# More row tiles of attention weights made ahead, a join taken five groups later, and a gradient product split around the last scan of a graph network

## What is computed

```python
def get_H(xx):
    z = xx @ W_fc.T
    e = jax.nn.sigmoid(jnp.concatenate([z[src], z[dst]], axis=-1) @ W_attn.T)
    emax = jax.ops.segment_max(e, dst, num_segments=n)
    w = jnp.exp(e - emax[dst])
    denom = jax.ops.segment_sum(w, dst, num_segments=n)
    h = jax.ops.segment_sum(w / denom[dst] * z[src], dst, num_segments=n)
    h1 = jax.ops.segment_sum((h @ W_encK.T + b_encK)[src], dst, num_segments=n)
    K = _mlp3(h1, K_w0, K_b0, K_w1, K_b1, K_w2, K_b2)
    ue = (h @ W_p1.T + b_p1)[src] + (h @ W_p2.T + b_p2)[dst]
    U = _mlp3(ue, U_w0, U_b0, U_w1, U_b1, U_w2, U_b2)
    return jnp.sum(jax.ops.segment_sum(K[src] * U, dst, num_segments=n))
dHdx = jax.grad(get_H)(x)
return dHdx @ J.T - dHdx @ D.T
```

## Time and profile before

| | |
|---|---|
| median of three runs | 9449.99 us (9428.79 to 9453.63) |
| profiled execution, time | 9455.71 us |
| its span | 9453.9 us |
| mean granted TensorE clock | 0.689 of full speed |
| PE busy | 4884.9 us (52%) |
| DVE busy | 4608.6 us (49%) |
| ACT busy | 2818.8 us (30%) |
| POOL busy | 5441.5 us (58%) |
| DRAM read and written | 1606.44 MB and 711.62 MB |

### The profile page before, as it was taken

The page is one execution under the profiler, slowest core; times in us unless marked ns, Lnnn a source line. Parts: engine busy times, 40 slices in busy tenths (PEclk is TensorE's granted clock), DMA queues, the critical chain, the costliest instruction groups (busy, mean ns, idle before and its releaser), DMA issues.

```text
span 9453.9 us, 77287 instructions
## 1 busy us (share of the span) xinstructions
PE 4884.9 (52%) x27914; PEld 2630.0 (28%) x27914; DVE 4608.6 (49%) x6100; ACT 2818.8 (30%) x2192; POOL 5441.5 (58%) x5420
## 2 busy tenths in 40 slices
PE   1000007999457777775577756344430035038976
PEld 0000006888113233231222222244430023032333
DVE  5789746777000000000398950488875410428870
ACT  0111110000000000000298940366657500429850
POOL 4777777777777777777610027688877777320000
PEclk6555555555578988987798975667665568559986
DMA  8887216444598989999799999455559848538767
GB/s 188 307 299 236 53 52 138 148 148 153 207 414 358 414 361 377 399 362 415 267 285 268 283 219 365 139 201 203 201 212 373 308 151 340 183 84 285 262 223 291
DMA packets 1203136, 2404.24 MB, mean 254 GB/s; under 512 B 566439, under 2 KB 818794, under 8 KB 1171354
## 3 DMA queue, kind: packets, MB, share of 16 engines
q1 hardware_dynamic: 996986, 2076.35, 61.8%
q0 software_dynamic: 187136, 170.29, 6.9%
q10 hardware_dynamic: 18720, 153.79, 4.2%
HBM read 1606.44 MB, written 711.62 MB: 245 GB/s over the span
## 4 chain that ended last, share of the span: by engine, by line
POOL 37%; DMA 26%; issue 12%; PE 11%; ACT 7%; ACTq 4%; DVE 2%; SPq 1%; DVEq 1%; POOLq 0%
POOL arena L486 18%; DMA arena<-cells_w 14%; POOL xd L489 9%; POOL cells_w L489 9%; DMA arena<-cells_c 8%; PE ps L699 5%; ACT arena L1031 3%; ACTq L1030 3%; ACT arena L1029 2%; PE ps L788 2%; DMA arena<-hot 1%; PE ps L880 1%; ACTq L2271 1%; PE ps L1162 1%; PE ps L1054 1%
## 5 line engine op out<-in xcount | busy, mean ns | idle before, releaser
L699 PE MATMUL ps<-arena 128*64 128x458 f32 (+2 forms) x7252 | 1345.0, 653 | 663.1 <-DMA arena<-cells_w 661.6
L486 POOL DMA_INDIRECT arena<-t_a,arena x832 | 947.9, 1139 | 1090.8 <-DMA t_a<-arena 837.7
L1054 PE MATMUL ps<-arena 128*33 128x400 f32 x6336 | 1173.1, 525 | 297.7 <-DVE arena L1049 289.8
L489 POOL DMA_INDIRECT sorted<-arena x832 | 843.8, 1014 | 289.9 <-issue 289.9
L489 POOL DMA_INDIRECT xd<-arena x832 | 832.0, 1000 | 260.9 <-issue 253.2
L717 DVE COPY carry<-ps 64x128 f32<-64x128 f32 (+1 forms) x5 | 1.5, 296 | 2006.1 <-PE ps L699 2006.1
L489 POOL DMA_INDIRECT cells_c<-arena x832 | 810.4, 974 | 293.5 <-issue 293.5
L486 POOL DMA_INDIRECT arena<-t_kv,idx x832 | 826.3, 993 | 258.7 <-issue 252.9
L489 POOL DMA_INDIRECT cells_w<-arena x832 | 813.7, 978 | 276.6 <-issue 276.6
L699 PEld LDWEIGHTS ps<-arena 128*64 128x64 f32 (+1 forms) x7252 | 425.5, 147 | 1579.0 <-issue 813.2
L1054 PEld LDWEIGHTS ps<-arena 128*33 128x33 f32 x6336 | 368.3, 115 | 1100.3 <-issue 662.9
(11 more groups left out here) (536 smaller groups left out, 9104.9 us busy)
## 6 DMA issues: line engine op xcount, KB each, us to landing
arena<-cells_w SPq DMA_DIRECT2D x245, 3200.0 KB
arena<-cells_c SPq DMA_DIRECT2D x294, 800.0 KB, 6.2
arena<-cells_turned SPq DMA_DIRECT2D x200, 800.0 KB, 8.2
cells_w<-arena SPq DMA_DIRECT2D x49, 3200.0 KB, 22.2
weighed_cells<-arena SPq DMA_DIRECT2D x68, 1600.0 KB, 14.2
arena<-weighed_cells SPq DMA_DIRECT2D x68, 1600.0 KB, 7.2
cells_c<-arena SPq DMA_DIRECT2D x50, 1600.0 KB, 5.8
cells_turned<-arena SPq DMA_DIRECT2D x100, 800.0 KB, 5.4
```

The lines of the kernel that those rows point to most:

```text
L486: return pool.indirect_dma_start(dst, None, table, bass.IndirectOffsetOnAxis(ap=index, axis=0))
L489: return pool.indirect_dma_start(table, bass.IndirectOffsetOnAxis(ap=index, axis=0), source, None)
L699: mm = pe.matmul(bank[base + k][g * f:(g + 1) * f, 0:m], rows_of, tile[:, g * width + at:g * width + at + m], start=first, stop=last, skip ...
L1054: last = pe.matmul(bank[4 * h + c][64 * kind:64 * kind + 33, 0:400], own[:, t, :], moving[:, 400 * c:400 * c + 400], start=t == 0, stop=do ...
```

## The change

Three tables or constants and two pieces of code change. `BEFORE` becomes 23 tiles spread over the 50 (0, 3, 5, 7, 9, 11, 14 and so on to 48). The join moves from group 29 to 34 of the puts and the fetch of `gk` from 37 to 42. ACT makes the tanh of the next piece between the exponential and the square of the present one. The gradient product is split: `DFM1` and `SUMS3` are multiplied right after the quarters, ahead of the join of the last scan, into four banks of PSUM that the scan's masks don't use; the product with `DFM2` is added after the scan.

```diff
-        BEFORE = range(0, NT, 3)
+        BEFORE = [t for t in range(NT) if t * 23 % NT < 23]
...
-        ALIAS_AT, XK_AT, GK_AT, HD_AT = 768, 15, 37, 29
+        ALIAS_AT, XK_AT, GK_AT, HD_AT = 768, 15, 42, 34
...
+        def gradient_pe(pe, source, weight, first):
+
+            if not first:
+                pe.wait_ge(S["fm_taken"], STEP["dhf"])
+            for t in range(NT):
+                to = bank[4 + t // 16][:, t % 16 * 32:t % 16 * 32 + 32]
+                g, at = t // (NT // 2), t % (NT // 2) * P
+                a = slice(64 * g, 64 * g + 64)
+                if t == NT // 2:
+                    last.then_inc(S["group_done"], 1)
+                    groups_done[0] += 1
+                    pe.wait_ge(S["group_done"], groups_done[0])
+                last = pe.matmul(to, source[a, at:at + P], weight[a, :], start=first and t % 16 == 0, stop=not first,
+                                 skip_group_check=True)
+                if first:
+                    last = pe.matmul(to, SUMS3[0:96, t * P:t * P + P], fold[32][0:96, 0:32], start=False, stop=False,
+                                     skip_group_check=True)
+                elif t % 16 == 15 or t == NT - 1:
+                    last.then_inc(S["fm_made"], 1)
...
+            tanh_act(0)
+            for i in range(len(todo)):
                 act.drain()
                 act.wait_ge(S["weighed"], base + max(0, 2 * i - 1))
-                act.activation(AHEAD_EXP, tanh, ACT.Exp, scale=0.5, bias=half[:]).then_inc(S["weights_made"], 1)
+                act.activation(AHEAD_EXP, AHEAD_TANH[i % 2], ACT.Exp, scale=0.5, bias=half[:]).then_inc(S["weights_made"], 1)
+                if i + 1 < len(todo):
+                    tanh_act(i + 1)
                 act.wait_ge(S["weighed"], base + 2 * i)
-                act.activation(AHEAD_SQUARE, tanh, ACT.Square).then_inc(S["weights_made"], 1)
+                act.activation(AHEAD_SQUARE, AHEAD_TANH[i % 2], ACT.Square).then_inc(S["weights_made"], 1)
...
-            for made, t, got in node_banks("dhf", 32, bank):
+            for made, t, got in node_banks("dhf", 32, bank[4:8]):
...
             quarters_pe(pe)
+            await_made(pe, "dh_made")
+            gradient_pe(pe, DFM1, WD1, True)
             ends_pe(pe, "dsum", OD, 64, bank[3])
             await_made(pe, "dd_made")
             to_features_pe(pe, "DD", nodes(DD, 64), 4)
-            await_made(pe, "dh_made")
-            to_nodes_pe(pe, "dhf", DFM1, 64, 32, lambda c: WD1[64 * c:64 * c + 64, :], bank,
-                        more=((DFM2, 64, lambda c: WD2[64 * c:64 * c + 64, :]), (SUMS3, 96, lambda c: fold[32][0:96, 0:32])))
+            gradient_pe(pe, DFM2, WD2, False)
```

More of the change, by code:

```diff
@@ L1094, in ahead_act, with tanh_act @@
             base = 4 * NS
-            for i, j, phase, t, h in ahead():
+            todo = list(ahead())
+            def tanh_act(i):
+                _, j, phase, t, h = todo[i]
                 if j % len(BEFORE) == 0 and h == 0:
                     act.wait_ge(S[f"other{phase}"], 16 * 2)
-                tanh = AHEAD_TANH[i % 2]
-                act.activation(tanh, piece_of(AHEAD_OTHER[phase], h), ACT.Tanh, bias=a_dst[:, t:t + 1])
+                act.activation(AHEAD_TANH[i % 2], piece_of(AHEAD_OTHER[phase], h), ACT.Tanh, bias=a_dst[:, t:t + 1])
+            tanh_act(0)
+            for i in range(len(todo)):
                 act.drain()
                 act.wait_ge(S["weighed"], base + max(0, 2 * i - 1))
-                act.activation(AHEAD_EXP, tanh, ACT.Exp, scale=0.5, bias=half[:]).then_inc(S["weights_made"], 1)
+                act.activation(AHEAD_EXP, AHEAD_TANH[i % 2], ACT.Exp, scale=0.5, bias=half[:]).then_inc(S["weights_made"], 1)
+                if i + 1 < len(todo):
+                    tanh_act(i + 1)
                 act.wait_ge(S["weighed"], base + 2 * i)
-                act.activation(AHEAD_SQUARE, tanh, ACT.Square).then_inc(S["weights_made"], 1)
+                act.activation(AHEAD_SQUARE, AHEAD_TANH[i % 2], ACT.Square).then_inc(S["weights_made"], 1)
         def ahead_dve(dve):
```

## The result

| | before | changed |
|---|---|---|
| median of the runs | 9444.13 us (4 runs, 9428.79 to 9453.63) | 9369.1 us (4 runs, 9359.15 to 9382.79) |
| ratio, 95% interval | | 0.9921 [0.9907, 0.9934] |
| profiled execution, span | 9455.71, 9453.9 us | 9359.15, 9357.3 us |
| mean granted TensorE clock | 0.689 | 0.692 |

A forecast was written before the change was run, and what follows sets the result against it. POOL's puts bound the time to 8142 us, then a serial scan, join and gradient product, then ACT in the back stage. Gains of 54.7 and 22, together 76.7 us, off the median 9449.99 gave 9373 us, range 9350 to 9424.

The forecast's parts named there:

- The gradient product: Between last scan and back stage: two of three products move ahead of the scan, 54.7 us less (50 to 55).
- The weights ahead: Stage making weights early: 24 more pieces at DMA's pace, 6.20 us each, ending about 7654; ACT's new order worth nothing.
- The join: Join among POOL's puts: five groups later, 7604.4 to 7709.3; DVE has 55 us left, less the last write; cost nothing.
- The cost of nothing for the last put: End of POOL's puts: same transfers in another order, so the last put still lands at 8142.78.
- The quarters: Before the last scan: preparation ends at 8137.4 against the last put at 8142.78, slack shrinking from 110 to 5.3 us.
- The bound upwards of 20 us: Most that late quarters were allowed to cost at the scan's start; the cost itself was taken as 0.
- The back stage: Two phases after the gradient product: PE leads at 5.44 us a tile; 10 and 12 less, together 22, at most 26.
- The rival of a limit at 349: Back stage gains nothing because DMA scaled to share 1 allows only 349 GB/s; time 9395 us, chance 0.16.
- Late quarters: Before the last scan: quarters overrun their 5.3 us slack; at 25 us delay the scan loses 20; 9393 us, chance 0.12.
- The slower case: Back stage held by DMA at 284 GB/s: 9509 us; slower than before if below 311 GB/s; chance 0.04.
- the change might not do what it says: Moved gradient products would run only after the scan, gaining nothing there; 9428 us with the back stage's gain, chance 0.03.
- the two middle cases: No gain in the back stage (0.16) and late quarters (0.12): 9393 to 9395 us, both together 9415.

## Why the prediction was right

**The gradient product: -54.7 forecast, -56.5 measured in the trace.** The row taken for the remaining product, `GK` with 21.80 us, was 2 us too dear: it took 19.74. The clock tells why. `GK` had run at 0.50 from end to end. Here the granted clock was 1.00 from 8398 to 8400, 0.99 from 8400 to 8402 and 0.50 from 8402 on, so the 0.83 in the window above is a mean of the two levels, 2.4 and 1.2 GHz. It fell though PE was busy without a break from 8400 to 8404, and stayed down while PE was busy for 5.94 of the 6 us from 8404. The first 50 matmuls took 8.83 us and the other 50 took 10.88. PE had been idle for 70.10 us ahead of the turn; the upper level came during the turn and was lost 2.3 us into the product. The prediction's "all through this product" is not exact for the same reason: the product before stood at 1.00 from 8414 to 8416 and at 0.50 only from 8418. By the rule of the Trainium skill that was weighed there (TensorE: Matmul & The Clock Gate, "What's actually happening") a busy array has 2.4 GHz, and the product would have taken an estimated 10.9 us; the trace speaks against it here as it did before.

**The weights ahead: 6.20 us a piece forecast, 6.23 measured;** ACT's order at nothing, and nothing it was, by the run with the old order.

**The join: "slack 55 less the last write".** DVE was idle 41.36 us before it, and POOL's loss in it was 3.2 us, as costed. The difference from 55 is not the write. DVE's pieces ended at 7652.7, as forecast (7654), but the join came some 15 us before 7709, because the puts began 18.4 us earlier. With the join back at 29 the loss is 70.7, which is the price that the move avoids. Two readings of POOL's stream were wrong without touching the sum: 750 of the 832 puts lie between 7082 and 8142 (they began at 6955.24), and from the first to the last put there are 885 indirect transfers, before and now, not 982. The cost of nothing for the last put was short by 1.8 us, the longer landing.

**The quarters: 5.3 us of slack forecast, 9.2 measured.** The positions have to be corrected for the puts, which began 18.4 us earlier in this execution: the end of the preparation, forecast at 8137.4, becomes 8119.0, and it was 8117.88; the last put, 8142.78 before, becomes 8124.4, and it had landed at 8127.06. So 1.1 us of the larger slack is the quarters' and 2.7 the last put's. The bound upwards of 20 us was not needed, and the run with two more groups shows that it was the right thing to bound: past the slack the scan starts as much later as the quarters end later.

**The back stage: -22 forecast, -22.0 measured, and part of that agreement is luck.** The prediction took four of the 100 pieces as done at 8543.04. It was five: the records before it are 32, 32 and 16, and a piece has 16. So 95 pieces were left, 258.4 us of PE's time and not 261.1, and its own rule with 2 us of waits gives 12.9 less, not 10. From the same piece on, phase 0 now runs from 8471.09 to 8731.46, 260.4 against 273.3: 12.9 less. (From its second tile, 8458.06, it is 273.4 against 286.7 from 8529.65: 13.3 less.) Phase 1 went from 285.8 to 277.0, 8.7 less, 12 forecast: "with 2 us of waits" was too hopeful there, where 5 are left. PE waits for DVE and DVE for counts. With the pieces counted right the sum of the two phases would have been 25; the miscount of 3 us one way and the waits of 3 us the other cancel in the 22. Waits from 8471 to 8725 us:

```profile
DVE arena L1063 <- DMA arena<-cells_turned: 51.5, 18, 4.9
...
PE ps L1074 <- DVE arena L1069: 6.2, 5, 2.1
```

That PE would lead with 5.44 us a tile was right (two pieces of 2.70 where nothing makes it wait), and that the reads "just fit" as well: share 0.99 to 1.01 at 350 to 358 GB/s. The rival of a limit at 349 fell. Its ground was that the rate ends at a share of 1 and grows in line with it; the share went to 1.05, and with 27 tiles the same reads reached 382. The 358 GB/s of the Trainium skill (DMA: Bandwidth & Descriptors, "Where 436 GB/s comes from"), with its estimate of 272 us a phase, could not be told from PE's own 272 at 23 tiles. At 27 tiles the windows of 374 to 382 GB/s are above it, and the measurement decides.

**The other rivals.** Late quarters (slack used up) appear at place 36 and not at 34. The slower case needed less than 311 GB/s; the stage moved 350 to 358. That the change might not do what it says is excluded by PE's rows at 8117.50 and 8172.59.

The chances do not quite add up: the forecast and the two middle cases are 0.88 by themselves, and they were given as 0.87 with a part of the rest.

What the sum left out is the 15.7 us at the start. The changed kernel's profiled execution, which shows them, is 10 us under its own median. Of the signs named ahead, "the scan's first load still within a few us of 8143" missed by 16 for this reason. That forecast and median agree to 4 us is finer than these runs can tell, as they spread over 24. Why the puts begin earlier in one execution than in another was not looked into.

## What to carry to other kernels

Cost an edit between fixed points of the trace (here from the turn to the first matmul, and from there to the second turn), not by where things stand on the clock: positions moved by 18 us between executions of the same code, while of those stretches the first agreed to 0.1 us between kernels with the same product, and the second to 5 us. Work that is moved ahead of a stage must be paid for on every queue that it passes: without the five groups by which the join was moved, POOL would have stood for 70 us behind DVE. And when work is made ahead and read back, stop where the engine that then leads has no waits left: here 20 of 50 tiles did for PE what 23 did, with fewer reads.

## What the runs showed of the hardware that was not expected

- TensorE's granted clock fell from 0.99 (8400 to 8402 us) to 0.50 (8402 to 8404) in the middle of a narrow product on which PE was busy without a break, and stayed at 0.50 while PE was busy for 5.94 of 6 us.
- The rate that the 16 DMA engines reach depends on the packets, and the share is no gauge of a limit. In the back stage, with packets under 2 KB, a share of 0.82 went with 286 GB/s, 1.01 with 358 and 1.05 with 380: it goes past 1, and the rate grows a little more than in line with it, so a rate scaled to a share of 1 is too low a limit. With 6,400 packets of 132 bytes in the queue, full engines moved 20 to 60 GB/s for some 7 us, and a row request of 1,600 KB that went out beside them took 21.76 us to land. DVE waited 13.14 us for the counts behind the two, 8.88 without the row in front of them, and not at all once the store went out later.
- The stage ahead of the puts varies: they began between 6936.84 and 6955.24 us in the profiled executions of kernels with the same code up to there. From the first put to the last it took 1183.2 to 1191.3 us where nothing made them wait.
